# Weaving feed-forward tiles between attention turns in a one-core transformer layer

## The chip, the cores and the metric

The kernel runs on one core of a Trainium2 chip. The metric is the device time of one execution in microseconds. Engines are named as the profile does: PE is TensorE (matmuls), PEld its weight loads, DVE VectorE, ACT ScalarE, POOL GpSimd, SP SyncE, whose queue issues all DMAs here.

## The reference

Input x is 4 x 1024 tokens of 256 numbers, float32. The layer is attention with 16 heads of 16 numbers and a gated feed-forward part of four weight layers, each between two layer norms:

```
q, k, v = linear(layernorm(x), alpha * sign(W))          # 256 -> 256 each
y = softmax(q k^T / 4) v
x1 = x + layernorm(linear(y, alpha * sign(Wp)))
n = layernorm(x1)
h = silu(n w1 * s1) * (n w2 * s2)                        # 256 -> 1024, ternary weights
h = gelu(h h1 * sh1)                                     # 1024 -> 1024
h = gelu(h h2 * sh2)                                     # 1024 -> 1024
out = x1 + layernorm(h w3 * s3)                          # 1024 -> 256
```

## The kernel before

The 4096 tokens are 8 blocks of 512 (BLK). Numbers that must keep float32 precision on fast matmuls are split into a high part (rounded to the fp32r type) and a low part (the rest), and each weight tile is multiplied with both. So a hidden tile of 128 outputs by 512 tokens is 16 matmuls of 512 columns, a tile of the first layers 4, and each part costs a copy (high) and a subtraction (low).

Three stages follow one another, each a block of its own with a barrier between them. `project` (L228 to L710) makes q, k and v of all tokens and stores them in DRAM scratch (`q_scr`, `k_scr`, `v_scr`); SP's queue carries these stores. `attention` (L713 to L953) takes 16 quads (four heads of one sequence). A quad has 16 groups, here called turns: a turn computes the scores of 4 heads for 128 keys by 512 queries (`scores`, L855: four matmuls with 50 rows, two side by side in the array, written to one of three `s_ps` buffers), two exponentials of 128 x 1024 on ACT (L909) and the weighted sums of the turn before (`pv`, L865: four calls of four passes' worth, shown as eight matmuls, into `y_ps`). The loads of quad g+2 are issued by SP when quad g has been copied out of `y_ps` (L789 to L804). Loads of q and k go into 16 partitions at a time (L145), twelve per quad, 128 KB each. In the same loop one sixteenth of the feed-forward weights per quad goes through DRAM scratch into `W`, which holds all of them, and DVE looks at their low bits (L936, L939) to choose between two forms of the feed-forward matmuls. DVE also inverts the softmax sums of the first block (L951) ahead of the last pair of quads.

`tail_ffn` (L956 on) then runs the 8 blocks in one step each: gate and product tiles (16), two hidden layers (8 tiles each, in groups of three with the contraction outermost), and the output. The projection of attention's y and the layer norms of block i+1 lie between the layers of block i. ACT applies silu and gelu straight from PSUM, tile by tile, and DVE makes high and low parts tile by tile. Six PSUM banks hold tiles. The first step and the last are written out, and the six between are a loop of two steps (`blocks`, L1068).

Every engine works through its own list in order and waits on semaphores. In `attention` PE issues per turn the two score pairs and then `pv` of the turn before.

## Time and profile before

| | us |
|---|---|
| median of 3 runs (lowest, highest) | 1326.21 (1323.45, 1326.53) |
| the profiled execution | 1326.26 |
| its span, first to last instruction | 1324.2 |
| PE busy | 1201.7 (91%) |
| ACT busy | 770.8 (58%) |
| DVE busy | 559.2 (42%) |
| granted PE clock, mean | 0.965 |

The span is one profiled execution. Busy times are averages over three stages with different limits, so they are read by stage: `project` until about 118 us, `attention` until about 611, `tail_ffn` from there. A busy PE is not PE at its peak, since matmuls are pipelined. A granted clock of 1.00 is 2.4 GHz and 0.50 is 1.2 GHz.

### The profile page before, as it was taken

To read this page: it belongs to the slowest core of one execution; us is meant where nothing else is said; L and a number is where in the kernel's file an instruction comes from. 1 tells how busy PE (TensorE), PEld (TensorE's weight loads), DVE (VectorE), ACT (ScalarE), POOL (GpSimd) and SP (SyncE) were. 2 spreads that over 40 slices of the span, in tenths; PEclk is the share of its full clock that TensorE was granted. 3 is DMA by queue.
4 is the path that set the end of the run, shared out by engine and by line. 5 is a ranking of instruction groups with operands and counts; after the bars stand their busy time and mean duration, and the time that the engine had idled before them with its cause. 6 is when DMAs were issued, how large, how long until landed. Compare 5 with 4: busy or idle time off the path is not lost.

```text
span 1324.2 us, 19216 instructions
## 1 busy us (share of the span) xinstructions
PE 1201.7 (91%) x6696; PEld 742.1 (56%) x6696; DVE 559.2 (42%) x1012; ACT 770.8 (58%) x920; POOL 38.3 (3%) x32
## 2 busy tenths in 40 slices
PE   4955999999999999965999999989999989999997
PEld 3742222222222222211788888878888878888886
DVE  7941111111111111143474756737557467475623
ACT  4954999999999999964423324324342243332421
POOL 5220000000000000000000000000000000000000
PEclk9975999999999999987899999999999989999999
DMA  4999577766677777722000100101001001010000
GB/s 154 372 278 273 132 137 149 161 124 124 138 141 136 137 135 158 159 71 63 2 33 0 32 32 14 52 2 33 32 1 64 1 21 45 1 32 1 10 7 16
DMA packets 49946, 115.06 MB, mean 87 GB/s; under 512 B 5856, under 2 KB 18528, under 8 KB 49880
## 3 DMA queue, kind: packets, MB, share of 16 engines
q1 hardware_dynamic: 49880, 114.17, 35.8%
q8 instruction: 42, 0.69, 0.2%
q14 instruction: 24, 0.20, 0.1%
HBM read 75.84 MB, written 49.81 MB: 95 GB/s over the span
## 4 chain that ended last, share of the span: by engine, by line
PE 51%; DVE 1%; issue 1%; ACT 0%; DVEq 0%; ACTq 0%
PE ffn_ps L1131 22%; PE ffn_ps L1132 22%; PE ffn_ps L1159 2%; PE ffn_ps L1160 2%; PE side_ps L1115 1%; PE side_ps L1124 1%; DVE ln_stats L1268 0%; DVE zn L1279 0%; DVE zn L1320 0%; DVE x L1303 0%; DVE x_lo L1310 0%; DVE zn L1296 0%; DVE zn L1293 0%; DVE zn L1330 0%; DVE ln_mean_var L1272 0%
## 5 line engine op out<-in xcount | busy, mean ns | idle before, releaser
L909 ACT ACTIVATE probs<-s_ps 128x1024 f32<-128x1024 f32 x512 | 471.5, 1122 | 25.7 <-PE s_ps L861 25.7
L1132 PE MATMUL ffn_ps<-h_lo,W 128*128 128x512 f32 x1024 | 401.5, 392 | 0.0
L1131 PE MATMUL ffn_ps<-h_hi,W 128*128 128x512 f32 x1024 | 401.5, 392 | 0.0
L870 PE MATMUL y_ps<-probs,v_st 128*32 128x512 f32 x2048 | 276.9, 613 | 34.7 <-DVE y_sb L944 10.4
L1222 ACT ACTIVATE hid<-ffn_ps,scales 128x512 f32<-128x512 f32 x128 | 80.9, 685 | 233.0 <-PE ffn_ps L1132 228.1
L1132 PEld LDWEIGHTS ffn_ps<-h_lo,W 128*128 128x128 f32 x1024 | 192.5, 188 | 42.2
L1131 PEld LDWEIGHTS ffn_ps<-h_hi,W 128*128 128x128 f32 x1024 | 192.5, 188 | 42.2
L861 PEld LDWEIGHTS s_ps<-q_st,k_st 50*128 50x128 f32 x1024 | 78.7, 187 | 235.9 <-ACT probs L909 225.2
L861 PE MATMUL s_ps<-q_st,k_st 50*128 50x512 f32 x1024 | 194.4, 454 | 13.4 <-issue 8.1
L936 DVE TENSOR_SCALAR low_bits<-W 128x1408 int32 (+1 forms) x16 | 14.3, 893 | 307.0 <-DMA W<-w_scr 307.0
L1344 DVE CAST h_hi<-hid 128x512 fp32r<-128x512 f32 x128 | 53.4, 417 | 184.0 <-ACT hid L1222 183.6
L1338 DVE TENSOR_TENSOR h_lo<-hid,h_hi 128x512 fp32r<-128x512 f32 x192 | 129.8, 683 | 1.0
L870 PEld LDWEIGHTS y_ps<-probs,v_st 128*32 128x32 f32 x2048 | 40.5, 108 | 143.5 <-ACT probs L909 124.5
L1131 PE MATMUL ffn_ps<-x_hi,W 128*128 128x512 f32 x256 | 104.7, 409 | 6.0 <-issue 3.6
L1132 PE MATMUL ffn_ps<-x_lo,W 128*128 128x512 f32 x256 | 103.9, 406 | 4.3 <-issue 4.3
L1352 DVE SCALAR_TENSOR_TENSOR hid<-ffn_ps,scales,gate 128x512 f32<-128x512 f32 x64 | 47.7, 750 | 58.0 <-ACT gate L1233 33.9
L130 DVE RECIPROCAL sums<-sums 128x256 f32<-128x256 f32 x32 | 54.5, 1730 | 28.9 <-DMA sums<-y_scr 28.9
L1233 ACT ACTIVATE gate<-ffn_ps,scales 128x512 f32<-128x512 f32 x64 | 43.6, 688 | 38.6 <-PE ffn_ps L1132 38.5
L1201 ACT ACTIVATE ln_std<-ln_mean_var,eps 128x4 f32<-128x4 f32 x24 | 7.1, 298 | 100.8 <-DVE ln_mean_var L1272 100.8
L1131 PEld LDWEIGHTS ffn_ps<-x_hi,W 128*128 128x128 f32 x256 | 50.3, 197 | 22.7 <-issue 8.8
L944 DVE COPY y_sb<-y_ps 128x512 f32<-128x512 f32 x32 | 21.9, 686 | 93.1 <-PE y_ps L870 93.1
L1159 PE MATMUL ffn_ps<-W,h_hi 128*128 128x256 f32 x256 | 59.7, 280 | 0.0
(103 smaller groups left out, 941.3 us busy)
## 6 DMA issues: line engine op xcount, KB each, us to landing
q_st<-q_scr SPq DMA_DIRECT2D x96, 128.0 KB, 6.7
k_st<-k_scr SPq DMA_DIRECT2D x96, 128.0 KB, 7.3
w_scr<-ffn_w SPq DMA_DIRECT2D x16, 704.0 KB, 13.2
W<-w_scr SPq DMA_DIRECT2D x16, 704.0 KB, 12.1
q_scr<-part SPq DMA_DIRECT2D x16, 512.0 KB, 7.7
k_scr<-part SPq DMA_DIRECT2D x16, 512.0 KB, 8.4
v_scr<-v_aug SPq DMA_DIRECT2D x8, 1024.0 KB, 8.2
v_st<-v_scr SPq DMA_DIRECT2D x16, 512.0 KB, 11.1
```

The source lines that it names most:

```text
L130: dve.reciprocal(sums, sums).then_inc(tail_in.inverted, 1)
L861: i = pe.matmul(s_ps[a % 3][:, hh, :], k_st[u][rows, pp, s * P:(s + 1) * P], q_st[u][rows, pp, tb * BLK:(tb + 1) * BLK], start=True, stop= ...
L870: i = pe.matmul(y_ps[32 * j:32 * (j + 1), tb * BLK:(tb + 1) * BLK], v_st[u][:, s, 32 * j:32 * (j + 1)], probs[m % 2][j // 2][:, j % 2, :], ...
L909: act.activation(probs[m % 2][pp][:, :, :], s_ps[a % 3][:, :, :], ACT.Exp, scale=SCALE).then_inc(probs_ready, 1)
L1131: pe.matmul(bank_of(t)[:, :], w, hi[:, k, :].bitcast(form), start=(k == 0), stop=False)
L1132: mm = pe.matmul(bank_of(t)[:, :], w, lo[:, k, :].bitcast(form), start=False, stop=last)
L1159: pe.matmul(dst, hi[:, k, tokens].bitcast(form), w, start=(k == 0 and a == 0), stop=False)
L1222: act.activation(hid[n % 3][:, :], bank_of(t)[:, :], ACT.Gelu, scale=scales[:, s:s + 1]).then_inc(gelu_done, 1)
L1233: act.activation(gate[n % 3][:, :], bank_of(2 * n)[:, :], ACT.Silu, scale=scales[:, S1_AT + n:S1_AT + n + 1]).then_inc(gate_done, 1)
L1338: dve.tensor_tensor(h_lo[a][:, n, :], hid[n % 3][:, :], h_hi[a][:, n, :].bitcast(F32), ALU.subtract).then_inc(h_lo_done, 1)
L1344: dve.tensor_copy(h_hi[a][:, n, :], hid[n % 3][:, :]).then_inc(hi2_done, 1)
L1352: dve.scalar_tensor_tensor(hid[n % 3][:, :], bank_of(2 * n + 1)[:, :], scales[:, S2_AT + n:S2_AT + n + 1], gate[n % 3][:, :], ALU.mult, AL ...
```

## The change

The stages `attention` and `tail_ffn` become one, `attend_and_feed`.

- Attention is cut into 32 steps of 8 turns, in the order of the token blocks: a step is four heads of one sequence for the 512 queries of one block. So k and v of a quad are loaded twice, q by halves (`load_k`, `load_q`, `load_v`). `s_ps` has two buffers instead of three, `y_ps` one bank instead of two.
- After the first 66 turns (LEAD) PE issues the feed-forward tiles of block i with turns of later blocks behind them: one turn behind each gate tile, one or two behind each product tile, six in each hidden layer, and one behind the projection and one behind the turning of x1. That makes 31 turns per block, so the 190 others are used up in block 6. Three banks (`f_ps`) hold tiles. All loops are written out.
- The hidden weights are no longer kept. They pass through `ring`, five chunks of 512 KB, one chunk per hidden tile, 16 per block. w1, w2 and w3 are kept (3.1 MB). All weights still go through DRAM scratch first: the kept ones and hid1 are copied there during `project`, hid2 (4.2 MB in four copies) at the start of attention.
- The look at the weights' low bits is one OR per chunk on DVE (`check`, 22 chunks), between the first turns.
- DVE takes every tile out of PSUM with its scale into `pre0` or `pre1`. ACT works on these in batches: silu is a tanh over four tiles at a time (and a multiplication on DVE), gelu runs over 4, 2 and 2 tiles. High and low parts are made in the same batches (4, 2, 2), all on DVE.

The core of the diff. In it stand, in this order, SP's two added copies in `project`, SP's `load_ring`, `attended` and order of work, PE's `attend` and `feed`, ACT's `feed`, and DVE's `attended` and what it does ahead of the first block:

```diff
+LEAD = 66
+GATE_TURNS = (1, 1, 1, 1, 1, 1, 1, 1)
+PROD_TURNS = (1, 1, 1, 1, 1, 1, 1, 2)
+HID_TURNS = (1, 1, 1, 1, 1, 0, 1, 0)
...
             sp.dma_start(const.scales[:, :], ffn_s).then_inc(small_loaded, 16)
+            sp.dma_start(w_scr[:, 0:W_KEPT], ffn_w[:, 0:W_KEPT]).then_inc(W.in_scr, 16)
             for u in range(2):
                 sp.wait_ge(norm_done, TILES * (u + 1))
                 load(2 + u, u)
+            hid1 = slice(W_KEPT, W_KEPT + HT * CHUNK)
+            sp.dma_start(w_scr[:, hid1], ffn_w[:, hid1]).then_inc(W.in_scr, 16)
...
+            def load_ring(n):
+                if n >= RING_ALL:
+                    return
+                if n >= RING:
+                    if n - RING < CHECK_ONLY:
+                        sp.wait_ge(checked, KEPT_CHUNKS + n - RING + 1)
+                    else:
+                        sp.wait_ge(tile_done, ring_user(n - RING) + 1)
+                c = chunk_of(n)
+                if c >= KEPT_CHUNKS + HT:
+                    sp.wait_ge(W.hid2_in_scr, 16 * HID2_COPIES)
+                sp.dma_start(ring[:, n % RING, :, :].rearrange("p k c -> p (k c)").bitcast(F32),
+                             w_scr[:, c * CHUNK:(c + 1) * CHUNK]).then_inc(ring_loaded[n % RING], 16)
+
+            def attended(n):
+                for turn in turns.take(n):
+                    if turn and turn % ST == 0:
+                        g = turn // ST - 1
+                        sp.wait_ge(y_copied, g + 1)
+                        sp.dma_start(y_scr[g * P:(g + 1) * P, :], y_sb[g % 2][:, :]).then_inc(y_stored[g % 2], 16)
+                        if g + 2 < STEPS:
+                            load_step(g + 2)
+                            load_shift(g + 2, g % 2, m_loaded[g % 2])
...
+            load_step(1)
             for u in range(2):
                 sp.wait_ge(stored[u], 16 * (STORES * BATCH + 1))
             sp.wait_ge(quads.shift_stored, 32)
+            sp.wait_ge(W.in_scr, 16 * 2)
+            sp.dma_start(W.kept[:, :].bitcast(F32), w_scr[:, 0:W_KEPT]).then_inc(W.loaded, 16)
+            for n in range(HT - RING):
+                load_ring(n)
+            for i in range(HID2_COPIES):
+                n = HT * CHUNK // HID2_COPIES
+                at = slice((KEPT_CHUNKS + HT) * CHUNK + i * n, (KEPT_CHUNKS + HT) * CHUNK + (i + 1) * n)
+                sp.dma_start(w_scr[:, at], ffn_w[:, at]).then_inc(W.hid2_in_scr, 16)
+            for n in range(HT - RING, RING + CHECK_ONLY):
+                attended(3)
+                load_ring(n)
+                if turns.done == STEPS_OF_BLOCK * ST + 1:
+                    load_x(0)
+                    load_y(0)
+            attended(LEAD - turns.done)
+            for i in range(BLOCKS):
+                feed(i)
...
+            def attend(turns, n):
+                for turn in turns.take(n):
+                    if turn < TURNS:
+                        scores(turn)
+                    if turn:
+                        pv(turn - 1)
...
+            def feed(form, turns, i):
+                pe.wait_ge(tile_read, turn_tile(i) + CT)
+                for n in range(HT):
+                    first_tile(form, tile_at(i, GATE, n), W1_AT, n)
+                    attend(turns, GATE_TURNS[n])
+                for n in range(HT):
+                    first_tile(form, tile_at(i, PROD, n), W2_AT, n)
+                    attend(turns, PROD_TURNS[n])
+                for m in range(HT):
+                    hidden_tile(form, i, 0, HID, m)
+                    attend(turns, HID_TURNS[m])
+                if not last(i):
+                    project_y(i + 1)
+                    attend(turns, 1)
+                for m in range(HT):
+                    hidden_tile(form, i, 1, hid2(i), m)
+                    attend(turns, HID_TURNS[m])
+                if not last(i):
+                    turn_x1(i + 1)
+                    attend(turns, 1)
+                out_tiles(form, i)
...
+            def feed(i):
+                for n in range(HT):
+                    attend(GATE_TURNS[n])
+                    if n == 2 and i:
+                        ln_std(ln_out(i - 1))
+                    if n == 5:
+                        tanh_of_gates(i, 0)
+                for n in range(HT):
+                    attend(PROD_TURNS[n])
+                    if n == 1:
+                        tanh_of_gates(i, 1)
+                for layer, stage in ((1, HID), (0, hid2(i))):
+                    for m in range(HT):
+                        attend(HID_TURNS[m])
+                        if m == 2 and layer == 0 and not last(i):
+                            ln_std(ln_z(i + 1))
+                        if m == 4:
+                            gelu(i, layer, stage, 0)
+                            if layer == 0 and not last(i):
+                                ln_std(ln_x1(i + 1))
+                        if m == 6:
+                            gelu(i, layer, stage, 1)
+                    gelu(i, layer, stage, 2)
+                    if not last(i):
+                        attend(1)
...
+            def attended(n):
+                for turn in turns.take(n):
+                    if turn and turn % ST == 0:
+                        g = turn // ST - 1
+                        dve.wait_ge(pv_done, turn)
+                        if g >= 2:
+                            dve.wait_ge(y_stored[g % 2], 16 * (g // 2))
+                        dve.tensor_copy(y_sb[g % 2][:, :], y_ps[:, :]).then_inc(y_copied, 1)
...
+            for n in range(CHUNKS):
+                check(n)
+                attended(2 + n % 2)
+                if n == 14:
+                    invert_sums(0, 0)
+                    invert_sums(0, 1)
+                elif n == 15:
+                    invert_sums(0, 2)
+                    invert_sums(0, 3)
+                elif n == 16:
+                    divide_y(0)
+                    high_of_y(0)
+                    low_of_y(0)
```

## Rows read from the trace of the kernel before

**Rows 1.** Stretches: us, busy and (instructions) per engine, PE clock, DMA share, GB/s

```profile
200.00:300.00 100.00, 93.84 (x650) 24.70 (x648) 14.51 (x15) 99.44 (x109) 0.00 (x0) 1.00 0.68 142
```

**Rows 2.** Timeline of PE in attention, full clock: start us, us, engine, line, what

```profile
131.34 0.73 PE L861 MATMUL s_ps<-q_st,k_st 50*128 50x512 f32 x4
132.14 1.06 PE L870 MATMUL y_ps<-probs,v_st 128*32 128x512 f32 x8
133.14 0.74 PE L861 MATMUL s_ps<-q_st,k_st 50*128 50x512 f32 x4
```

**Rows 3.** Timeline, the first turns of attention, at low clock

```profile
118.60 1.65 PE L861 MATMUL s_ps<-q_st,k_st 50*128 50x512 f32 x6 [8.13 <-issue]
...
126.30 1.22 PE L861 MATMUL s_ps<-q_st,k_st 50*128 50x512 f32 x4
...
129.31 1.11 PE L861 MATMUL s_ps<-q_st,k_st 50*128 50x512 f32 x4
```

**Rows 4.** The chain that ended last, in order: start us, us, what

```profile
633.79 0.79 PE ffn_ps L1131
...
711.51 0.87 PE side_ps L1124 x8
763.60 1.90 PE side_ps L1115 x16
...
794.81 0.87 PE side_ps L1124 x8
...
878.10 0.88 PE side_ps L1124 x8
886.24 1.61 issue
...
967.31 0.87 PE side_ps L1124 x8
...
1314.41 1.30 DVE zn L1320 x2
```

**Rows 5.** Timeline at the two holes, with [idle before <-releaser]

```profile
568.62 6.59 DVE L130 RECIPROCAL sums<-sums 128x256 f32<-128x256 f32 x4 [28.90 <-DMA sums<-y_scr]
...
579.66 1.94 PE L870 MATMUL y_ps<-probs,v_st 128*32 128x512 f32 x8 [10.40 <-DVE y_sb L944]
...
611.58 1.06 ACT L1206 ACTIVATE x_hi<-y 128x1024 fp32r<-128x1024 f32 x1 [2.73 <-PEq L723]
```

**Rows 6.** Stretches of 5 us in the projection

```profile
25.00:30.00 5.00, 4.22 (x21) 2.68 (x20) 3.21 (x7) 4.81 (x6) 0.00 (x0) 1.00 0.00 0
...
45.00:50.00 5.00, 4.52 (x24) 3.32 (x25) 4.85 (x9) 5.00 (x5) 0.00 (x0) 1.00 1.06 409
```

**Rows 7.** Stretches of 2 us: loads of q and k, of W, of y and sums

```profile
316.00:318.00 2.00, 1.90 (x20) 0.45 (x12) 0.00 (x0) 2.00 (x4) 0.00 (x0) 1.00 1.11 125
...
322.00:324.00 2.00, 1.90 (x14) 0.62 (x16) 0.59 (x1) 2.00 (x3) 0.00 (x0) 1.00 0.83 344
...
564.00:566.00 2.00, 1.89 (x20) 0.46 (x12) 0.00 (x0) 2.00 (x4) 0.00 (x0) 1.00 0.52 194
```

**Rows 8.** SP's queue, first and twelfth load of a quad; page: KB, us to landing

```profile
303.48 0.35 SPq L145 DMA_DIRECT2D q_st<-q_scr  x1
...
308.93 0.37 SPq L145 DMA_DIRECT2D k_st<-k_scr  x1
...
y_scr<-y_sb SPq DMA_DIRECT2D x16, 512.0 KB, 3.3
```

**Rows 9.** Groups of instructions: line, engine, what, xcount | busy us, mean ns | idle

```profile
L1338 DVE TENSOR_TENSOR h_lo<-hid,h_hi 128x512 fp32r<-128x512 f32 x142 | 96.0, 683 | 0.8
L130 DVE RECIPROCAL sums<-sums 128x256 f32<-128x256 f32 x24 | 41.1, 1733 | 0.0
L1344 DVE CAST h_hi<-hid 128x512 fp32r<-128x512 f32 x93 | 38.7, 416 | 119.9 <-ACT hid L1222 119.4
L1352 DVE SCALAR_TENSOR_TENSOR hid<-ffn_ps,scales,gate 128x512 f32<-128x512 f32 x48 | 35.7, 750 | 44.4 <-ACT gate L1233 23.7 <-PE ffn_ps L1132 20.7
L1320 DVE TENSOR_TENSOR zn<-ffn_ps,out_row 128x512 f32<-128x512 f32 x12 | 7.7, 686 | 22.6 <-PE ffn_ps L1160 22.6
L1284 DVE TENSOR_TENSOR x_lo<-y,x_hi 128x1024 fp32r<-128x1024 f32 x6 | 7.3, 1218 | 0.0
...
L587 ACT ACTIVATE part<-qk 128x2048 fp32r<-128x2048 f32 x8 | 15.2, 1902 | 18.9 <-DMA v_scr<-v_aug 18.9
```

**Rows 10.** ACT's timeline in a feed-forward block: a table load and what follows

```profile
738.83 0.30 ACT L1201 ACTIVATE ln_std<-ln_mean_var,eps 128x4 f32<-128x4 f32 x1 [1.31 <-DVE ln_mean_var L1272]
744.48 1.28 ACT L1222 ACT_TABLE_LOAD   x1 [5.36 <-PE ffn_ps L1132]
745.78 1.84 ACT L1222 ACTIVATE hid<-ffn_ps,scales 128x512 f32<-128x512 f32 x3
```

More of the change, by code:

```diff
@@ L710, in _, with __init__, take @@
             pe.matmul(bound_ps, ones[:, :], bound[:, :], start=True, stop=True).then_inc(bound_spread, 1)
[L713 to L722 removed]
+class Turns:
+    def __init__(self, done=0):
+        self.done = done
+    def take(self, n):
+        first, self.done = self.done, min(self.done + n, TURNS + 1)
+        return range(first, self.done)
@@ L912, in _, with most_of_rows @@
+            attend(48)
+            ln_std(ln_z(0))
+            attend(5)
+            ln_std(ln_x1(0))
+            attend(LEAD - turns.done)
+            for i in range(BLOCKS):
+                feed(i)
+            ln_std(ln_out(BLOCKS - 1))
         @block.vector
         def _(dve):
-            wide = dve.value_load(const.wide_range[:, :], min_val=0, max_val=1)
-            with dve.If(wide):
+            def most_of_rows():
                 with dve.Fori(0, QUADS) as g:
@@ L1396 @@
+            low_bits()
+            norm_x1(0)
+            attended(5)
+            any_low_bits()
+            attended(3)
+            split_x2(0)
+            attended(LEAD - turns.done)
+            dve.wait_ge(halved, 1)
+            for i in range(BLOCKS):
+                feed(i)
+            f = BLOCKS - 1
+            stats_out(f)
+            ln_var(ln_out(f))
+            norm_out(f)
+            add_out(f)
 def kernel(L0_attn_x, L0_attn_Wq, L0_attn_bq, L0_attn_Wk, L0_attn_bk, L0_attn_Wv, L0_attn_bv, L0_attn_Wp,
```

1134 lines of the change are left out of this document (581 added, 553 removed).

## Prediction

> **What bounds the kernel now.** I read the busy times by stretch first. In the attention stage ScalarE is busy 99.4 of 100 us with 109 exponentials, so a turn (two exponentials, four score matmuls, eight weighted-sum matmuls) takes 2 x 100/109 = 1.84 us [rows 1]. TensorE shows as 94% busy there, but that figure holds pipeline fill. The timeline gives its real need: weighted sums issued at 132.14 are followed by scores at 133.14 (1.0 us), and the scores of 131.34 last 0.73 us [rows 2]. A turn needs 1.73 us of TensorE, I take 1.72, and only about 0.12 us of each turn is free. At the low clock a turn takes 3.0 us (scores at 126.30 and at 129.31) [rows 3].
>
> Next the chain that ended last. It is TensorE from 633.8 to 1314.4 us: a feed-forward block goes from one turning of x1 (711.51) to the next (794.81) in 83.3 us with no gap; the block from 878.10 to 967.31 takes 89.2, with an issue gap of 1.6 us at a loop's jump back and low clock after it, and there are two blocks of this kind, so 12 us; the tail behind the last matmul is 9.8 us [rows 4]. Between the stages lie two holes. Four reciprocals of 6.6 us in all stand ahead of the copy that frees y_ps, and TensorE waits 10.4 us for that copy, some 15 us with the low clock behind it [rows 5]. And the first feed-forward matmul comes 22 us after the first step of the tail (611.58 to 633.79), about 28 with the ramp [rows 4, 5].
>
> So apart from the projection, the time is 470 us of a ScalarE-bound stage, 663 of a TensorE-bound stage, and about 56 of holes.
>
> **What weaving removes.** The holes go: 15 + 28 us, and 12 us of loop jumps, as the new body has no loop (if straight code starved the sequencer it would cost some of that back; nothing in the rows suggests it). Of 256 turns, 66 come before the first feed-forward tile (LEAD) and 190 are woven. A woven turn costs TensorE 1.72 instead of 1.84, a gain of 23 us in all; the bounds are 1.65 (the score group overlaps the tile ahead) and 1.84 (two more changes of operand shape cost what is free now). Were nothing else to happen: scores start at 118.6, the fifth turn at 129.3 [rows 3], 62 turns more bring 243.4, with the first projection and turning (1.9 + 0.9, rows 4, and a wait) 246; then 190 x 1.72 = 327, 663 of tiles, 9.8 of tail: 1246. This is the floor that the change aims at. The rest is what it puts in the way.
>
> **The projection stage.** Two copies to the DRAM scratch are added on SP's queue, 3.1 and 4.2 MB. At 409 GB/s [rows 6] they take 8 and 10 us of all engines. The queue is empty from 25 to 30 us and full afterwards [rows 6], so the first hides and part of the second too; half of the first q is no longer loaded. I take +2 us, bounds 0 and +10.
>
> **The lead: 66 turns that now carry more transfers and more checks.** A step is now 8 turns, 14.7 us, and still loads all of k and v. Loads into 16 partitions at a time run at 125 GB/s with every DMA engine busy, against 344 GB/s for W [rows 7]. So a step's load is 1.18 MB at 125 (9.4 us), v 1.6, y 0.8: 12 us of queue, and its issue alone is 6 us for twelve transfers (303.48 to 309.3) [rows 8]. It is issued only when the step before last has been copied out of y_ps, which, since scores stand ahead of the old step's last weighted sums on TensorE, is after the wait for the load ahead of it. So this chain, about 2 us to the last weighted sum, 0.7 of copy, 12 of queue, 2 of landing (y_scr: 3.3 us for 512 KB, which is 1.5 at 344 GB/s) [rows 8], must fit in 14.7: I take 16.5 per step (bounds 14.7 and 19). Before, it had 29 us.
> The Trainium skill (SBUF — State Buffer, Door 1: The DMA port swizzle) says that 16 partitions reach 4 of 16 ports and were measured at 104 GB/s; the trace agrees with 125. By that page partitions 64 and up lie on other ports; the new order alternates between the two halves from one transfer to the next, and if neighbours overlap, the rate could double, which is the first rival.
>
> The DVE checks and SP's order add stalls of their own.
> - y_ps has one buffer now. The copy of step 0 stands behind checks 0 to 3 on DVE, and check 0 waits for all kept weights: step 1's load takes the queue from 119 to 130.5, 3.1 MB at 344 GB/s until 140, landing 142. Then 0.7 + 3 x 1.25 (1218 ns for 1024 columns, and a wait) + 0.7 [rows 9] gives 147, while TensorE wants it at 140 (129.3 and 5.5 turns).
> - SP sends ring chunk 3 only when all of hid2 (4.2 MB) is in scratch: 140 + 4.6 (three chunks) + 12.2, and 2 of landing, is 159. Behind this wait stand two chunks and the load of step 2: it lands at 169 to 178, where turn 16 was due at 151. Both together: +20 us.
> - At turns 16 and 24 SP must also wait for two checks that follow the copy (2.5 us): 19.5 instead of 16.5, so +10 for the two steps. Three plain steps: +5.
> - y of block 0 is asked for after turn 32. Such loads run with half the DMA engines, at 194 GB/s (564 to 566) [rows 7], behind the load of step 5. DVE meets the reciprocals in turn 37, waits for y, spends 4 x 1.73 [rows 9] and 2.5 of checks, and only then copies y_ps at turn 40. This is the hole of rows 5 again: +15 us (10 to 18).
> Sum of the lead: 246 + 2 + 20 + 10 + 5 + 15 = 298 us at the first tile; bounds 262 and 325.
>
> **Six woven blocks** (31 turns each): 83.3 + 31 x 1.72 = 136.6 us. In gate and product phases a tile (0.92) and a turn make 2.64 us, against 1.84 of ScalarE; since s_ps has two buffers and not three, work put between exponentials reaches TensorE at once. A square root between exponentials costs two table loads of 1.28 and 0.3 = 2.9 us on ScalarE, a tanh over 2048 columns 1.9 (by the 1902 ns of a copy of that size) [rows 9, 10]. After the 0.8 us of slack a turn: 1.9 for the root, 1.0 for each tanh, 4 per block. Gelus in batches sit where a hidden tile of 3.6 us gives cover: its load, 1.9, and the load back are 4.5 us of ScalarE (6 with a root) between turns 9 us apart, free. DVE has about 66 us of work in 140, free on average; y_ps copies can queue behind a 2.3 us operation, which I put in the range. Ring chunks (0.5 MB, 1.6 us) are asked for four tiles ahead, about 20 us, and land in at most as much when a step's load is ahead: free, at most 2 us a block. Step loads in the gate phase have 8 x 2.64 = 21 us for 16.5 to 19: free. So 140.5 per block (bounds 135 and 150), 843 in all. The transfers of a block (17 MB, 84 us of queue) fit.
> What each table switch costs is told by row: the gelu behind the table load of 744.48 starts at 745.78, so 1.3 us and nothing more [rows 10].
> **Two blocks without cover.** Four turns are left for block 6. There the new way of leaving PSUM costs: DVE takes gates (8 x 0.69), silu over SBUF (2 x 2.3), products (8 x 0.75), the high and low parts (3.3 and 5 us or so), and the layer norm of the block before (4.6): 28 us where TensorE has 14.5 in the two first phases of block 7 [rows 9]. Of this the last 3 us lie beside the next layer: +11. Layer seams, where gelu, high and low of the last two tiles follow each other (0.7, 1.1, 0.7, 1.2) with only 2.7 us of tiles beside them: +2 each, +4. Low clock in those gaps: +2. Block 7: 80.4 + 17 = 97. Block 6: 83.3 + 7 + 8 = 98. Bounds 88 and 106 for each.
>
> **Sum.** 298 + 843 + 98 + 97 + 9.8 = 1346 us of span; the profiled execution lies 2.1 us above its span and equals the median of the runs: 1348.
>
> **Rivals.**
> 1. *The lead's transfers keep up* (30%). The alternating halves run side by side, so a step fits its 14.7 us, hid2 is there earlier, and only the wait of DVE for y stays: 272 at the first tile. With a turn at 1.66 and 2 us of ScalarE per block, 6 x 137 = 822, and 94 + 88 for the last two: 1288, and 1265 to 1320 with the bounds. For it: issue needs only 6 us per step. Against it: before, the halves alternate as well, after every second transfer, and the rate is 125.
> 2. *All is covered* (10%): the floor of 1246, with 2 us for the projection and the 2.1, up to 1265. Against it: the reciprocals' hole needs a y load that the order of SP does not allow earlier.
> 3. *ScalarE stays the bound inside the weave* (12%), on the slow side. If tanh needs a table of its own (two loads more, 2.6 us for each of two) and a turn still costs 1.84, a block is 83.3 + 57 + 9 = 149.5 and the sum 1346 + 6 x 9 = 1400. It decides once work between exponentials exceeds the 0.8 us of slack, which each root and tanh does; what is open is the amount.
> 4. The gains and losses meet (6%): 1322 to 1330. 2% for something not seen, such as starved straight code, slower. That the change does nothing isn't possible here: turns and tiles stand in one order on TensorE.
> The forecast, 1348 (its own range 1330 to 1388), has 40%.
>
> **How the numbers follow.** Within 0.3% is about what a measurement of this kernel can tell from no change. Faster: rivals 1 and 2, 40%. Same: 6%. Slower: 54%. The range from 1262 to 1395 leaves out most of rival 2 and half of rival 3. The likeliest sign's own range stands above.
>
> **What would show it.** In the profile after: first feed-forward tile at about 298 us, with TensorE waits for loads of k and q and for y_sb of 8 to 25 us at turns 9, 16 and 41 (a start before 275 is rival 1); DMA share near 1 from 120 to 290; woven blocks 140 us apart, with waits on exponentials only behind tanh and root (150 us apart is rival 3, with 16 table loads a block); the last two blocks at 98 us with TensorE waiting for DVE in gates and products; no idle stretch between the stages. The prediction fails most easily on the lead, where a few waits make 50 us.

## The result, and the profile after

| | before | after |
|---|---|---|
| median, us (lowest, highest) | 1324.83 (1322.87, 1326.53) | 1435.51 (1431.86, 1438.83) |
| the profiled execution | 1326.26 | 1431.86 |
| its span | 1324.2 | 1430.2 |
| PE busy | 1201.7 (91%) | 1271.9 (89%) |
| ACT busy | 770.8 (58%) | 778.0 (54%) |
| DVE busy | 559.2 (42%) | 737.2 (52%) |
| granted PE clock, mean | 0.965 | 0.946 |

The changed kernel is slower: ratio 1.0829, 95% interval 1.0803 to 1.0855, against 1348 us forecast with a range up to 1395. The medians of before come from the runs beside those of after.

The timeline of PE in the profile after holds the milestones (start us, us, engine, line, what, [idle before <-releaser]). First the waits of the lead, which is every turn before the first feed-forward tile:

```profile
142.84 1.08 PE L1053 MATMUL y_ps<-probs,v_st 128*32 128x512 f32 x4 [3.55 <-DVE y_sb L1276]
...
168.43 0.79 PE L1042 MATMUL s_ps<-q_st,k_st 50*128 50x512 f32 x2 [11.30 <-DMA q_st<-m_scr]
...
187.70 0.79 PE L1042 MATMUL s_ps<-q_st,k_st 50*128 50x512 f32 x2 [1.53 <-DMA v_st<-v_scr]
...
241.75 1.08 PE L1053 MATMUL y_ps<-probs,v_st 128*32 128x512 f32 x4 [15.54 <-DVE y_sb L1276]
...
262.68 0.80 PE L1042 MATMUL s_ps<-q_st,k_st 50*128 50x512 f32 x2 [2.46 <-ACT probs L1193]
...
308.29 0.77 PE L1097 MATMUL f_ps<-x_hi,w_kept 128*128 128x512 f32 x1 [4.04 <-issue]
```

The first tile comes at 308.3 (forecast 298). The waits at turns 9, 17 (16 in the forecast's count) and 41 stand where they were forecast, and the hole of [rows 5] is back as the 15.5 us wait.

Then a gate tile and a turn in the middle of the weave, at full clock. The period from one `s_ps` to the next is 2.77 us:

```profile
1081.54 0.72 PE L1042 MATMUL s_ps<-q_st,k_st 50*128 50x512 f32 x4
1082.19 1.06 PE L1053 MATMUL y_ps<-probs,v_st 128*32 128x512 f32 x8
1083.19 0.50 PE L1097 MATMUL f_ps<-x_hi,w_kept 128*128 128x512 f32 x1
1083.53 0.39 PE L1098 MATMUL f_ps<-x_lo,w_kept 128*128 128x512 f32 x1
1083.76 0.39 PE L1097 MATMUL f_ps<-x_hi,w_kept 128*128 128x512 f32 x1
1083.99 0.40 PE L1098 MATMUL f_ps<-x_lo,w_kept 128*128 128x512 f32 x1
1084.31 0.73 PE L1042 MATMUL s_ps<-q_st,k_st 50*128 50x512 f32 x4
```

Scores take 0.66 us and weighted sums 1.00, somewhat less than in [rows 2] (0.73 and 1.0). But the tile takes 1.12, where it needed 0.92 before: the first matmul of 128 rows behind the weighted sums holds the next back by 0.34 us instead of 0.23, and the scores start 0.32 behind the last.

Third, the out tiles of a block:

```profile
1201.82 0.38 PE L1128 MATMUL f_ps<-w_kept,h_hi 128*128 128x256 f32 x1
...
1205.25 0.58 PE L1128 MATMUL f_ps<-w_kept,h_hi 128*128 128x256 f32 x1 [2.69 <-DVE x_lo L1386]
1205.62 0.41 PE L1129 MATMUL f_ps<-w_kept,h_lo 128*128 128x256 f32 x1
...
1211.57 0.28 PE L1128 MATMUL f_ps<-w_kept,h_hi 128*128 128x256 f32 x1
```

Four matmuls, a wait of 2.7 us for the subtraction that empties the bank of the turned x1, then matmuls 0.21 us apart until 1211 and 0.12 from there (full clock). From 1201.82 to the next tile the out tiles need 13.3 us, where the last block, with no such wait, needs 7.7 (1413.12 to 1420.85). Not every block pays this much. The same 2.7 us wait stands in all six woven blocks, but their out tiles take 13.3, 12.1, 10.6, 12.1, 13.3 and 13.3 us, 12.4 in the mean. In the third of them the clock did not fall at all. The stretches of the third and the sixth (the same columns as in the stretches below):

```profile
755.06:765.70 10.64, 7.95 (x69) 7.74 (x65) 4.88 (x8) 2.67 (x3) 0.00 (x0) 1.00 0.03 10
1201.82:1215.10 13.28, 10.59 (x68) 10.38 (x65) 4.85 (x8) 2.66 (x3) 0.00 (x0) 0.74 0.02 8
```

Why the clock falls behind one of these waits and not behind the other stays open.

Stretches of the span (us, busy and (instructions) of PE, PEld, DVE, ACT, POOL, clock, DMA share, GB/s): four of the lead, the last woven block, the two blocks behind it.

```profile
120.00:160.00 40.00, 31.96 (x180) 8.60 (x180) 8.55 (x8) 29.87 (x32) 0.00 (x0) 0.88 0.96 314
160.00:200.00 40.00, 28.72 (x148) 7.73 (x148) 9.77 (x9) 23.38 (x25) 0.00 (x0) 0.70 0.69 180
200.00:240.00 40.00, 24.97 (x158) 6.92 (x156) 9.60 (x8) 26.41 (x28) 0.00 (x0) 0.85 0.68 174
240.00:290.00 50.00, 41.09 (x233) 12.19 (x233) 24.51 (x46) 38.51 (x41) 0.00 (x0) 0.84 0.53 106
...
1064.90:1215.10 150.20, 145.47 (x782) 85.45 (x781) 79.71 (x114) 88.97 (x86) 0.00 (x0) 0.98 0.42 112
1215.10:1325.80 110.70, 99.07 (x467) 74.96 (x466) 76.66 (x111) 30.73 (x27) 0.00 (x0) 0.95 0.31 98
1325.80:1420.90 95.10, 86.81 (x386) 68.89 (x384) 53.83 (x69) 16.06 (x12) 0.00 (x0) 0.96 0.21 67
```

The DMA share is near 1 only until 160, and in the woven block it is 0.42: transfers bound some places of the lead, not the weave. ACT is busy for 89 of 150 us there, so neither does it. The six woven blocks run from 308.3 to 1215.1, 151 us each (forecast 140.5), block 6 takes 110.7 (98) and block 7 95.1 (97).

### The profile page after: what moved, and what is told of

The parts are those of the page before. It is cut to its first block, busy times and chain, and to the rows that moved or that the text cites. A ratio compares the mean times of both kernels' runs of the same rounds, so it can differ in the third digit from the quotient of the medians.

```text
span 1430.2 us, 17019 instructions
## 1 busy us (share of the span) xinstructions
PE 1271.9 (89%) x6696; PEld 748.3 (52%) x6696; DVE 737.2 (52%) x1076; ACT 778.0 (54%) x764; POOL 34.8 (2%) x32
## 4 chain that ended last, share of the span: by engine, by line
PE 62%; ACT 9%; DVE 8%; DMA 5%; SPq 4%; issue 3%; ACTq 0%; DVEq 0%
PE f_ps L1110 16%; PE f_ps L1111 15%; PE y_ps L1053 11%; PE s_ps L1042 8%; ACT probs L1193 7%; PE f_ps L1097 3%; DMA sums<-y_scr 3%; PE f_ps L1128 3%; PE f_ps L1129 2%; DVE h_lo L1453 2%; PE f_ps L1098 2%; DMA w_scr<-ffn_w 2%; SPq L117 1%; DVE h_hi L1445 1%; SPq L126 1%
## 5 line engine op out<-in xcount | busy, mean ns | idle before, releaser
L1193 ACT ACTIVATE probs<-s_ps 128x1024 f32<-128x1024 f32 x512 | 494.0, 1024 | 386.4 <-PE s_ps L1042 384.5
L1110 PE MATMUL f_ps<-h_hi,ring 128*128 128x512 f32 x1024 | 413.7, 404 | 14.9 <-DVE h_lo L1453 9.0
L1111 PE MATMUL f_ps<-h_lo,ring 128*128 128x512 f32 x1024 | 404.0, 395 | 0.0
L1110 PEld LDWEIGHTS f_ps<-h_hi,ring 128*128 128x128 f32 x1024 | 194.1, 190 | 129.1 <-DVE h_lo_raw L1433 53.8
L1433 DVE TENSOR_SCALAR h_lo_raw<-f_ps,scales 128x512 f32<-128x512 f32 x128 | 94.9, 741 | 240.7 <-PE f_ps L1111 240.4
L1111 PEld LDWEIGHTS f_ps<-h_lo,ring 128*128 128x128 f32 x1024 | 194.0, 189 | 39.6
L1097 PE MATMUL f_ps<-x_hi,w_kept 128*128 128x512 f32 x256 | 115.5, 451 | 8.8 <-issue 4.0
L1453 DVE TENSOR_TENSOR h_lo<-h_lo_raw,h_hi 128x1024 fp32r<-128x1024 f32 (+1 forms) x72 | 113.6, 1577 | 1.7
L1098 PE MATMUL f_ps<-x_lo,w_kept 128*128 128x512 f32 x256 | 103.4, 404 | 0.0
L1128 PE MATMUL f_ps<-w_kept,h_hi 128*128 128x256 f32 x256 | 74.5, 322 | 20.5 <-DVE x_lo L1386 20.4
L1414 DVE TENSOR_SCALAR h_lo_raw<-f_ps,scales 128x512 f32<-128x512 f32 x64 | 47.6, 748 | 82.4 <-PE f_ps L1098 81.4
L1129 PE MATMUL f_ps<-w_kept,h_lo 128*128 128x256 f32 x256 | 72.5, 314 | 0.0
```

Source lines behind the costliest of these rows:

```text
L1097: pe.matmul(bank(tile)[:, :], w, x2_hi[:, k, :].bitcast(form), start=(k == 0), stop=False)
L1098: i = pe.matmul(bank(tile)[:, :], w, x2_lo[:, k, :].bitcast(form), start=False, stop=(k == CT - 1))
L1110: pe.matmul(bank(tile)[:, :], w, h_hi[layer][:, k, :].bitcast(form), start=(k == 0), stop=False)
L1111: mm = pe.matmul(bank(tile)[:, :], w, h_lo[layer][:, k, :].bitcast(form), start=False, stop=(k == HT - 1))
L1128: pe.matmul(dst, h_hi[0][:, k, tokens].bitcast(form), w, start=(k == 0 and a == 0), stop=False)
L1129: mm = pe.matmul(dst, h_lo[0][:, k, tokens].bitcast(form), w, start=False, stop=(k == HT - 1 and a == per_bank - 1))
```

## The experiments

Ratios are to the runs of before on the same chip; 1% is 13 us. The theory after reading the trace: the weave costs TensorE more per turn than ScalarE's bound did; the out tiles' wait and its low clock come from VectorE's order; and the two score buffers slow the turns outside the weave. Kernels whose label begins with b are made from before, those with a from after.

### Two score buffers in the kernel before

```diff
-        s_ps = [... for i in range(3)]
+        s_ps = [... for i in range(2)]
```

> The kernel before with two score buffers instead of three, nothing else. My theory now: in the kernel after, an unwoven turn costs about 2.03 us instead of 1.84 because the scores of a pair can no longer run ahead of the exponentials; so this kernel should be 256 x 0.19 = 49 us slower than before, near 1375 us, with turns of 2.0 to 2.05 us and ScalarE at about 90% busy in the middle of attention. The rival: the third buffer is unused slack and the 2.03 us of the lead comes from the loads and the checks on VectorE beside it. Then this kernel stays within 5 us of before (1321 to 1331) with turns of 1.84.

Measured 1356.77 us, ratio 1.0228 (1.0199 to 1.0258), +30 us. The stretch of [rows 1] in this kernel, and a stretch of the next kernel's long lead:

```profile
200.00:300.00 100.00, 95.89 (x610) 26.62 (x608) 11.41 (x12) 96.16 (x102) 0.00 (x0) 1.00 0.68 130
```

```profile
300.00:400.00 100.00, 95.37 (x600) 26.44 (x600) 4.14 (x6) 95.69 (x100) 0.00 (x0) 1.00 0.64 128
```

102 exponentials in 100 us make a turn 1.96 us, against 1.84. 256 x 0.12 = 31 us is the whole difference. The mechanism holds, at 0.12 instead of my 0.19: the 2.03 that I had read in the lead held some low clock and waits. In the long lead an undisturbed unwoven turn takes 2.0 us (100 exponentials). In its 100 us the kernel with two buffers has TensorE wait 3.7 us for exponentials (22 times) and ScalarE 2.7 us for scores (17 times), against 1.0 and 0.6 us (3 times each) before.

### Nothing woven

```diff
-LEAD = 66
+LEAD = 257
```

> The kernel after with all 256 turns ahead of the first feed-forward tile: the same pieces, nothing woven. My theory: a woven turn costs TensorE about 1.87 us, an unwoven one 2.03, so the 190 turns that move to the lead cost 190 x 0.16 = 30 us more, and six blocks lose their cover and cost what block 7 shows (95.1 us, against 83.3 + 5.7 us of out-tile stall = 89, so 6 each, 36 us). Sum: 1435 + 66 = about 1500 us (1485 to 1520), first tile near 308 + 190 x 2.03 = 694. The rival, that weaving itself loses (ScalarE's turns still bound the woven stretches, table loads between them), expects that undoing it costs nothing or helps: 1435 or less. If a woven turn really cost the 1.72 us of my forecast, the lead would lose 59 us and the sum would be 1530 or more.

Measured 1507.23 us, ratio 1.1363 (1.1292 to 1.1433), +71 us on after. First tile at 687.8, seven blocks of 101.3 us in the mean (out tiles at 775.9 to 1484.9). So weaving as such helps this set of pieces, by 71 us, and the rival falls. Some 17 us of it are turns (190 x 0.09, from 2.0 unwoven to 1.91 woven), the rest is cover: a block takes 101.3 us alone and 151.1 - 31 x 1.91 = 91.9 in the weave. The loss to before must then lie for the greater part in the pieces that the weave needs and in the stalls of this order. That is a reading of the sums; no run weaves the pieces of before. One part of the price shows here without any turns in the way: a block of 101 us has the same matmuls as the one of 83.3 us in [rows 4]. By the timeline its first tiles take 22.7 us for 14.7 (they wait for VectorE's batches), the out tiles 14.3 for 7.7, the hidden layers 61.4 for 58.2.

### High and low parts of x1 made earlier

```diff
-                for part in (1, 2):
-                    high(i, 2, part)
-                    low(i, 2, part)
+                high(i, 2, 1)
+                low(i, 2, 1)
                 if not last(i):
                     split_x2(i + 1)
+                high(i, 2, 2)
+                low(i, 2, 2)
```

> The kernel after with one edit on VectorE: the high and low parts of the turned x1 (which empty the PSUM bank that the third out tile needs) are made before the last pair of high and low parts of the hidden layer, not after. My theory: the out tiles of a block take 13.3 us instead of 7.7 because TensorE waits 2.7 us for that subtraction and then runs at the low clock; the edit brings them back to about 8 us, 7 blocks x 5.6 = 39 us less, 1396 us (1392 to 1405). Rival A: the wait is the price of the hidden layer's own last high and low parts, which the edit only delays: TensorE waits 2 to 3 us for those in its place, ahead of the first out tile, and the time stays at 1430 to 1440. Rival B: the low clock there does not follow from the wait; then only 7 x 2.7 = 19 us are gained (1416).

Measured 1406.62 us, ratio 1.0604 (1.0516 to 1.0693), 30 us less by the difference of the ratios. PE's timeline at the out tiles of a block:

```profile
1032.62 0.38 PE L1128 MATMUL f_ps<-w_kept,h_hi 128*128 128x256 f32 x1
...
1034.19 0.39 PE L1128 MATMUL f_ps<-w_kept,h_hi 128*128 128x256 f32 x1 [0.82 <-DVE x_lo L1386]
1034.41 0.28 PE L1129 MATMUL f_ps<-w_kept,h_lo 128*128 128x256 f32 x1
```

A wait of 0.8 us is left and no low clock follows it: the out tiles take 8.8 us in each of the six woven blocks (10.6 to 13.3 in after). Block 6 keeps a wait of 2.4 us with low clock, and 12.0 us (13.8 in after, with a wait of 4.2). Both rivals fall. No other wait takes the place. For the second the times alone would not do, since the interval leaves 18 to 42 us of gain; but in the traces the out tiles of the seven blocks take 24 us less while their waits shrink by 13, so 11 us of low clock went with the waits. The 30 us are less than my 39, because a wait stays and because not every block of after had the full 13.3.

### hid2's copies: later, spread, or none

Of four copies of 1 MB: the first edit puts the load of step 2 ahead of the four copies; the second gives each copy its semaphore and issues it two chunks ahead of its use; the third reads hid1's chunks in place of hid2's.

```diff
+            attended(STEPS_OF_BLOCK * 2 + 1)      # later
             for i in range(HID2_COPIES):
...
-                    sp.wait_ge(W.hid2_in_scr, 16 * HID2_COPIES)
+                    sp.wait_ge(W.hid2_in_scr[(c - KEPT_CHUNKS - HT) // 2], 16)      # spread
...
-                    sp.wait_ge(W.hid2_in_scr, 16 * HID2_COPIES)
+                    c -= HT      # none
```

> The kernel after with SyncE's order changed: the load of step 2 is issued ahead of the four copies of hid2 into the scratch, not behind them. My theory: the 11.3 us wait of the 17th turn for q and k (and the low clock behind it) comes from this order; it goes, and the first feed-forward tile starts 10 to 14 us earlier (294 to 298), the total falls by as much, 1422 us (1418 to 1428). The rival: the load of step 2 was late because its own buffers came free late and 16-partition loads are slow; then it lands only some 3 us earlier, and the copies of hid2, now after it, delay the loads of steps 3 and 4 by what is gained: 1432 to 1440.

> The kernel after with the four 1 MB copies of hid2 spread between the ring's first chunks on SyncE's queue, two chunks ahead of their use, each with a semaphore of its own, so that no chunk waits for all four. The same bytes. If the price of hid2 is its order, the wait at the 17th turn shrinks from 11.3 to below 4 us, none over 4 us takes its place, and the first tile comes 8 to 12 us earlier (total near 1425). If it is its bytes, waits at the 17th and 25th turns together stay at 10 us or more and the total within 5 us of 1435.

> The kernel after without the four copies of hid2 into the scratch: the ring's chunks of hid2 are read from hid1's place in the scratch, so the second hidden layer multiplies with the first one's weights (that part of the computation is changed), with the same tiles, turns and bytes through the ring. The run before this one showed that moving these copies behind a step's load only moves TensorE's wait from the 17th turn (11.3 us) to the 25th (14.3 us). If the 8.4 MB of traffic are what the lead pays for, the waits at both places go (to under 2 us each), the first feed-forward tile comes 10 to 14 us earlier (294 to 298 us) and the total is 1421 to 1426 us. If the lead is bound by the step loads into 16 partitions alone, as my forecast's 16.5 us per step has it, a wait of some 8 us stays at the 17th or the 25th turn and less than 6 us are gained (1430 or more).

| | ratio (interval) | median us | waits at turns 17, 25, 33 | first tile |
|---|---|---|---|---|
| after | 1.0829 | 1435.5 | 11.3, 1.5, none | 308.3 |
| later | 1.0823 (1.0788 to 1.0859) | 1435.7 | none, 14.3, 2.4 | 306.6 |
| spread | 1.0774 (1.0701 to 1.0846) | 1426.5 | 4.6, 6.0, 2.8 | 309.5 |
| none | 1.0696 (1.0636 to 1.0756) | 1416.3 | none, 3.3, 3.7 | 302.2 |

The kernel with the later copies, at the start of turn 25:

```profile
188.53 1.22 PE L1043 MATMUL s_ps<-q_st,k_st 50*128 50x512 f32 x4 [14.33 <-DMA q_st<-m_scr]
```

My theory fell for the later copies (the rival's 1432 to 1440 holds) and for the first tile of the other two. For the spread copies the waits at turns 17 and 25 stay at 10.6 us together, as the reading by bytes had it; with none, neither reading's waits came out whole. Order moves the wait and spreads it; with the same bytes the three waits add up to 12.8, 16.7 and 13.5 us. Without the copies they add up to 7.0, and the first tile comes 6 us earlier, not 10 to 14. The waits of 3.3 and 3.7 us that remain fit the step chain of the forecast (a load is issued only when the step before last has left y_ps); that part is argued, not isolated. The rest of the 12 us between the spans (1417.9 and 1430.2) arises in the blocks behind, whose code is the same. Four of these 6 us lie in the out tiles, which behind the same waits of 2.7 us had less low clock (four blocks near 12.2 us and two of 10.7). Blocks with the same code differ by up to 8 us within one kernel (147.5 to 155.7, from one projection to the next, in after), so differences of some us between kernels, such as that of the spread one, whose lead gained nothing, prove nothing about the lead.

### The sums of block 0 inverted later

```diff
-                if n == 14:
+                if n == 16:
                     invert_sums(0, 0)
...
-            attend(turns, 45)
+            attend(turns, 47)
             project_y(0)
```

> The kernel after with block 0's softmax sums inverted on VectorE two checks later (behind checks 16 and 17 in place of 14 and 15), so that they have landed and the copy that frees y_ps does not stand behind the wait for them; TensorE projects block 0 two turns later. My theory: TensorE's wait of 15.5 us at the 41st turn, low clock after it, is this order on VectorE. It goes, the first feed-forward tile comes 12 to 17 us earlier (292 to 296 us), the total falls to 1418 to 1423. The rival: the transfers are what is late (sums, y and a step's load share the queue), so another wait takes its place, at the next step's load or at the projection, and the first tile comes within 5 us of 308.

Measured 1426.10 us, ratio 1.0770 (1.0717 to 1.0824); first tile at 306.5, so the lead gained 2 us and the rival was right. VectorE in this kernel, and TensorE at the projection:

```profile
238.82 1.75 DVE L1312 RECIPROCAL sums<-sums 128x256 f32<-128x256 f32 x1 [11.21 <-DMA sums<-y_scr]
```

```profile
249.84 0.58 PE L1079 MATMUL f_ps<-signs_p,x_hi 128*128 128x256 f32 x1 [10.93 <-DVE x_lo L1324]
```

The copy of y_ps is now in time, and SyncE at once issues the next step's load; the sums, asked for at 220, land at 238.8 instead of 232.2, and the projection waits. The data itself was late: in after, the chain of waits has `219.95 12.24 DMA sums<-y_scr`.

### A woven turn without ScalarE

```diff
                     hidden_tile(form, i, 0, HID, m)
+                    if last(i) and 1 <= m <= 6:
+                        idle_turn(True)       # 4 score matmuls, 8 of weighted sums
...
                     hidden_tile(form, i, 1, hid2(i), m)
+                    if last(i) and 1 <= m <= 6:
+                        idle_turn(False)      # 4 score matmuls
```

> The kernel after with matmuls that nobody reads added in block 7, where ScalarE's exponentials have ended: a whole turn (four score matmuls, eight of weighted sums) behind each of tiles 1 to 6 of the first hidden layer, the four score matmuls alone behind tiles 1 to 6 of the second. It measures what a woven turn costs TensorE with no ScalarE in it. My theory (each change of the operands' shape costs about 0.1 us): a period of tile and turn is 3.64 + 1.655 + 0.24 = 5.5 us, scores 0.66, weighted sums 0.99 and the tile behind them 3.88, the same as in the woven blocks; with scores alone 3.64 + 0.66 + 0.1 to 0.2 = 4.4 to 4.5. The rival, that in the woven blocks ScalarE or the semaphores set the 5.5 us: here the period is 3.64 + 1.72 = 5.36 or less, the tile back at 3.64. Read from the trace alone; the total is about 12 x 1.3 = 15 us above 1432.

PE's timeline in block 7, a whole turn and a tile, then scores alone:

```profile
1358.39 0.74 PE L1119 MATMUL s_ps<-q_st,k_st 50*128 50x512 f32 x4
1359.06 1.06 PE L1123 MATMUL y_ps<-probs,v_st 128*32 128x512 f32 x8
1360.06 0.50 PE L1110 MATMUL f_ps<-h_hi,ring 128*128 128x512 f32 x1
1360.39 0.39 PE L1111 MATMUL f_ps<-h_lo,ring 128*128 128x512 f32 x1
...
1363.94 0.73 PE L1119 MATMUL s_ps<-q_st,k_st 50*128 50x512 f32 x4
...
1406.10 0.73 PE L1119 MATMUL s_ps<-q_st,k_st 50*128 50x512 f32 x4
1406.76 0.50 PE L1110 MATMUL f_ps<-h_hi,ring 128*128 128x512 f32 x1
...
1410.60 0.73 PE L1119 MATMUL s_ps<-q_st,k_st 50*128 50x512 f32 x4
```

The period is 5.55 us with nothing to wait for, and a hidden tile alone takes 3.64 (of the 83.3 us block, 16 hidden tiles have 58.2). A woven turn therefore costs TensorE 1.91 us by its matmuls alone: 0.67 + 1.00 + 0.24 that the tile becomes longer. With scores alone the tile grows by 0.20. So most of the extra comes with leaving and re-entering the tile's shape once, whether the scores alone or both groups stand between. The rival, that ScalarE sets this period, falls. What inside the array costs the 0.2 us (the weights' load, the row or column groups) these runs do not separate. Block 7 took 111.5 us for 95.1, and the twelve groups by their own prices come to 6 x 1.91 + 6 x 0.86 = 16.6: nothing of them was hidden. That this single run took 1442.87 us, only 7 more than after, comes from the blocks ahead, whose code is the same: block 7 started at 1320.2 and not at 1325.8.

### Everything mended that could be

Split early, copies spread, the inversion three checks and the projection seven turns later than in after:

```diff
-LEAD = 66
+LEAD = 74
...
-            attend(turns, 45)
+            attend(turns, 52)
             project_y(0)
```

> The kernel after with its avoidable stalls mended together: high and low parts of the turned x1 ahead of the hidden layer's last (29 us less when alone), hid2's copies spread (the waits at the 17th and 25th turns were 4.6 and 6.0 us for 11.3 and 1.5), block 0's sums inverted four turns later still and its projection behind the 52nd turn in place of the 45th, with LEAD 74. When the sums were inverted only two checks later, they landed at 238.8 us in place of 232.2 and TensorE waited 10.9 us at the projection in place of 15.5 for y_ps. My theory: the data of block 0 is what is late, so a projection that asks for it 7 turns later waits under 1 us; first tile at 308 - 13 (y) - 2 (hid2) + 15 (8 more turns of the lead) = 308 with 182 turns left to weave (15 us less). Sum: 1435 - 29 - 13 - 2 = 1391 us (1383 to 1400). What is left over before (66 us) is then the price of the design: woven turns at 1.90 us for 1.84, unwoven ones at 2.01, layers without cover. The rival, that weaving pays once the stalls are gone: 1350 or less.

Measured 1400.95 us, ratio 1.0553 (1.0519 to 1.0587). The projection waits for nothing, but the first tile comes at 315.2 instead of 308, with a new wait of 4.6 us for v at the 49th turn, and two woven blocks hold a wait of the kind that the lead had: VectorE meets the next block's sums before they have landed. In the timeline of after, VectorE and TensorE in block 2:

```profile
684.91 1.75 DVE L1312 RECIPROCAL sums<-sums 128x256 f32<-128x256 f32 x1 [19.31 <-DMA sums<-y_scr]
...
687.28 0.79 PE L1110 MATMUL f_ps<-h_hi,ring 128*128 128x512 f32 x1 [4.20 <-DVE h_lo_raw L1433]
```

In the mended kernel this wait is 3.6 us in block 2 and 1.6 in block 1, with low clock behind the first. That accounts for part of the 10 us by which I missed. The rival (1350 or less) is out.

### The kernel before with its holes mended

```diff
-            with eng.Fori(0, BATCH - 1) as b:
+            for b in range(BATCH - 1):
...
-            for part in range(INVERT_PARTS):
-                invert_sums(dve, tail_in, 0, part)
-            divide_y(dve, tail_in, 0)
-            pair(QUADS // 2 - 1)
+            pair(QUADS // 2 - 1, True)      # two reciprocals behind each copy of y_ps, then the division
```

> The kernel before with only the feed-forward loop written out. Theory: the two blocks of 89.2 us become 83.3 each, 12 us less, 1313 us (1311 to 1317), with no issue gap at 886. Rival: fetching straight code costs it back: issue gaps elsewhere, 1320 or more.

> The kernel before with only the inversion of block 0's sums spread behind the last pair's copies of y_ps. Theory: TensorE's wait of 10.4 us near 568 us goes and nothing takes its place: 1310 us (1307 to 1314). Rival: what VectorE had done there now lies in the seam between the stages (the first step of the tail waits for the divided y), and the feed-forward's first matmul comes as late as before: 1322 to 1326.

> The kernel before with two of the holes mended that the change was to fill: the inversion of block 0's sums spread behind the last pair's copies, and the loop of the feed-forward stage written out. My theory: the 10.4 us wait for y_ps with its low clock (15 us) and the two loop jumps (12 us) go without any weaving: 1325 - 27 = 1298 us (1293 to 1306). Rivals: the sums' inversion moved behind the attention lengthens the 22 us seam by what it saves (1313), or straight code starves TensorE's sequencer and costs the 12 us back (1310 or more).

| | median us | ratio (interval) |
|---|---|---|
| loop written out | 1312.08 | 0.9891 (0.9861 to 0.9921) |
| sums inverted later | 1313.08 | 0.9898 (0.9868 to 0.9929) |
| both | 1299.33 | 0.9793 (0.9767 to 0.9820) |

Both holes go, and they add up. With the loop written out every block's turning of x1 stands 83.3 us behind the last (700.23, 783.51, 866.80, 950.09 in the kernel with both), with no issue gap between. In the kernel with only the sums later, the 10.4 us wait of [rows 5] is gone, and the first tile comes at 618.6 for 633.8. So 27 of the 55 us of holes that the weave was to fill are had without it, and this version is faster than both kernels.

## Why the prediction was wrong

The sign had 54%, but the size fell outside the range. Two steps of the sum carry most of it: a woven turn was priced at 1.72 us and measured 1.91, and the out tiles, put at no stall, lost 36 us over seven blocks to waits for VectorE and low clock. The terms one by one:

| term | forecast | measured | difference |
|---|---|---|---|
| first tile | 298 | 308.3 | +10 |
| six woven blocks | 843 | 906.8 | +64 |
| block 6 | 98 | 110.7 | +13 |
| block 7 | 97 | 95.1 | -2 |
| tail and the rest beside the span | 11.9 | 11.0 | -1 |
| sum | 1348 | 1431.9 | +84 |

**The price of a turn in the weave** (+5.9 us a block, 35 in all). I took 1.72 us, from matmuls in attention [rows 2], and wrote that two more changes of operand shape would at worst bring it to 1.84. The rows show 1.91: (22.7 - 1.9 of waits)/31 = 0.67 for scores, 0.997 for sums, and the tiles of a woven block take 18.9 + 61.4 us for 14.7 + 58.2, 0.24 per turn. The bound was the mistake: [rows 2] said what a change between scores and sums costs, and nothing about entering and leaving the 128-row tiles. I closed the range at the point where the gain would be zero, though no row did. With 1.91 a woven turn has no gain over ScalarE's 1.84: the 190 of them cost 13 us more than before, where I had booked 23 of gain.

**The out tiles** (+4.8 us a block in the mean of the six, 5.6 where the low clock lasted longest; the edit that moves `split_x2` gave back 30 us in all). I had put them at no stall. In VectorE's list `split_x2` stands behind two high and two low parts of 128 x 1024, 0.7 + 1.2 + 0.7 + 1.2 us, and the third out tile needs its bank. In the profile after, beside the out tiles from 1201.82:

```profile
1200.06 0.68 DVE L1445 CAST h_hi<-h_lo_raw 128x1024 fp32r<-128x1024 f32 x1
1200.78 1.23 DVE L1453 TENSOR_TENSOR h_lo<-h_lo_raw,h_hi 128x1024 fp32r<-128x1024 f32 x1
...
1202.64 1.23 DVE L1453 TENSOR_TENSOR h_lo<-h_lo_raw,h_hi 128x1024 fp32r<-128x1024 f32 x1
1203.78 0.68 DVE L1384 CAST x_hi<-f_ps 128x512 fp32r<-128x512 f32 x1
1204.50 0.69 DVE L1386 TENSOR_TENSOR x_lo<-f_ps,x_hi 128x512 fp32r<-128x512 f32 x1
```

The diff's order said so; I had looked at this seam for the high and low parts only in the blocks without cover. In seven blocks together the out tiles took 36 us more than at block 7's 7.7 us each: 20 us of waits and 15 of low clock.

**The lead** (+10). Right in its places: waits for y_sb at turns 9 and 41, for a step's load at turn 17, the 15 us. Its size came near by two errors that partly cancel. I put the stalls at 50 us, and 2 more in the projection, which took no longer (scores start at 118.4 for 118.6). They came to 31.9 and, with low clock, about 45. (The lead less its projection and turning takes 186.6 us; without its waits above 1 us, 40.9, the 65 turns after the start take 2.24 each against 2.0. That is 16 us of low clock, of which the first turns' 3 stood in the forecast's base.) Missing was the third score buffer's price, 66 x 0.16 = 10 us, the two roots between exponentials (2 x 2.46) and the 4 us issue gap at the jump into the feed-forward part. The cause that I gave for the hole at turn 41 was half the matter: behind VectorE's order stood a late transfer, and mending the order alone gave 2 us.

**The rest of a woven block.** Root and tanh: waits on exponentials of 1.9 us in the last one, forecast 4. (The forecast's own terms, 2.9 - 0.8 for the root and twice 1.9 - 0.8 for tanh, would give 4.3.) The late sums, which the forecast did not have in the weave: 1.7 us in block 1 and, with low clock, 6.7 in block 2. Low clock at the start of block 0: 2. So 5.9 + 4.8 - 2.1 + 1.4 for the sums + 0.4 for the start make 10.4 of the 10.6 us a block.

**The last two blocks.** First tiles 22.7 us for 14.7 (+8, forecast +11) and hidden layers 64.6 for 58.2 in block 7, which was right within 2 us. Block 6 has the out tiles' stall on top, 13.7 us for 7.7, and had been given 8 for what cost 13 (first tiles 24.9, hidden layers 61.4).

**The rivals.** The first (the lead's transfers keep up) did not occur, though the later steps of the lead came nearer to it than to my 16.5 us: one wait of 1.5. The second didn't. The third, ScalarE as the bound with a table of tanh's own, is refuted by the count in the last woven block:

```profile
L1193 ACT ACT_TABLE_LOAD x6 | 7.7, 1283 | 8.9 <-PE s_ps L1042 8.9
...
L1211 ACT ACT_TABLE_LOAD x4 | 5.1, 1283 | 0.1
L1198 ACT ACT_TABLE_LOAD x3 | 3.8, 1283 | 0.1
```

```profile
214.00:216.00 2.00, 1.89 (x14) 0.53 (x12) 0.00 (x0) 1.96 (x3) 0.00 (x0) 1.00 1.05 129
216.00:218.00 2.00, 1.95 (x14) 0.53 (x12) 0.00 (x0) 1.89 (x3) 0.00 (x0) 1.00 1.03 123
```

All DMA engines are busy at 129 and 123 GB/s, as with the 125 of [rows 7]. So the rate did not double. In the weave the loads were not what bound, with a DMA share of 0.42.

The price of a change of ScalarE's tables was right. Where no idle time stands around it, in the lead of the profile after, the root between exponentials takes two loads of 1.28 us and its own 0.3, and nothing else lies between:

```profile
256.74 1.94 ACT L1193 ACTIVATE probs<-s_ps 128x1024 f32<-128x1024 f32 x2 [0.25 <-PE s_ps L1042]
258.69 1.28 ACT L1198 ACT_TABLE_LOAD   x1
259.99 0.30 ACT L1198 ACTIVATE ln_std<-ln_mean_var,eps 128x4 f32<-128x4 f32 x1
260.31 1.28 ACT L1193 ACT_TABLE_LOAD   x1
```

## What to carry to other kernels

Before weaving work of two operand shapes on TensorE, price the change of shape from both sides, with a probe that has nothing else in it (here 0.24 us a group, which was more than the 0.12 us of slack that the weave was to use), and do not end a bound where the gain would be zero. Count what is given up for the weave (a score buffer, tile by tile evacuation, kept weights) as costs at full price. Here the two blocks without cover cost about 28 us, the 66 turns of the lead 10 and hid2's copies 6 in the lead, against 13 for the woven turns; VectorE's order ahead of the out tiles cost another 30. When a wait goes back to an engine's order, look at when its data lands; if both are late, mending the order gives nothing.

## What the runs showed of the hardware

- A group of narrow matmuls (four of 50 rows, alone or with eight of 32 columns behind them) between 128 x 128 tiles costs 0.20 to 0.24 us beyond its own length: the first matmul back in the tile's shape holds up the next by 0.34 us instead of 0.23, and the first narrow one starts 0.32 behind the last.
- The same wait of 2.7 us, with the same instructions around it, was followed by 1.2 GHz in five of six woven blocks (matmuls of 256 columns 0.21 us apart for 0.12) and by none in one. The low clock lasted about 7 us in three of them, its start lying within the wait, and 3.4 us in two. After the six 0.8 us waits of the kernel with the early high and low parts there was none.
- Straight code of six blocks did not starve TensorE's sequencer: in the kernel before with its loop written out the blocks run 83.3 us apart with no issue gap, where each loop jump, with the low clock behind it, had cost 6 us (89.2 for 83.3).
- Two score buffers instead of three cost 0.12 us a turn, with TensorE and ScalarE both shown as 96% busy in that stretch; their waits for each other grow from 1.0 and 0.6 us to 3.7 and 2.7 in 100 us.
- Loads into 16 partitions that change sides with each transfer ran at 123 to 129 GB/s with all DMA engines busy, no faster than the 125 before.
- A load of ScalarE's tables between busy instructions took 1.28 us and left no other gap.
